# Routed stage: expert masks of chunks 1 to 3 spread by DMA instead of by TensorE and ScalarE, and the one-hot transposes moved to the turn before

## What is computed

```python
logits = gelu(xf @ w_r1 + b_r1) @ w_r2 + b_r2          # 8 experts
top_p, top_i = top_k(softmax(logits), 2)               # two experts a token
for _ in range(2):
    ctx = concatenate([integrated, v])                 # 256 features
    hidden = gelu(ctx @ expert_w1[i] + expert_b1[i])   # 64 wide, for each chosen expert
    ctrl = hidden @ expert_w2[i] + expert_b2[i]        # alpha, beta, gate: 3 x 128
    x_r, v_r = step(ctrl, integrated, v, mu)           # weighted by top_p, and summed
    ...                                                # the same for a shared expert; mixed
    integrated = integrated + halt * refined * integration_weight
```

## Time and profile before

| | us |
|---|---|
| median of 3 runs | 866.23 (865.97 to 867.63) |
| the profiled execution, its own time | 868.9 |
| its span, first to last instruction | 867.1 |
| PE busy in the span | 828.4 (96%) |
| DVE busy | 630.4 (73%) |
| ACT busy | 567.4 (65%) |
| GpSimd (POOL) busy | 286.4 (33%) |

### The profile page before, as it was taken

One profiled execution on the slowest core, in us unless ns is written; L12 is line 12 of the kernel. 1 busy time (PEld: TensorE's weight loads), 2 busy tenths in 40 slices (PEclk: granted clock), 3 DMA queues, 4 the chain that ended last, 5 costly groups with the idle time before them and its releaser, 6 DMA issues.

```text
span 867.1 us, 20115 instructions
## 1 busy us (share of the span) xinstructions
PE 828.4 (96%) x7204; PEld 571.1 (66%) x7204; DVE 630.4 (73%) x1587; ACT 567.4 (65%) x1569; POOL 286.4 (33%) x586
## 2 busy tenths in 40 slices
PE   9999999999999999999999999999999989899986
PEld 8887888888889976544444444444467665676652
DVE  5677776777776655685785766775989876789876
ACT  3666677677777676866545586445477779677664
POOL 4355444444554442200000000002156520334355
PEclk9999999999999999999999999999999999999999
DMA  8700000000000000000000000000000000000000
GB/s 340 156 2 2 1 2 1 2 2 1 2 1 2 2 1 2 1 1 0 1 0 1 0 1 0 1 0 1 1 27 3 4 3 1 2 4 3 3 15 37
DMA packets 7821, 13.55 MB, mean 16 GB/s; under 512 B 4342, under 2 KB 5036, under 8 KB 7468
## 3 DMA queue, kind: packets, MB, share of 16 engines
q1 hardware_dynamic: 7724, 12.27, 4.5%
HBM read 11.22 MB, written 1.05 MB: 14 GB/s over the span
## 4 chain that ended last, share of the span: by engine, by line
PE 59%; DVE 20%; POOL 10%; issue 6%; ACT 4%; DMA 0%; DVEq 0%; POOLq 0%; SPq 0%; ACTq 0%
PE psum L1551 10%; PE psum L767 6%; POOL rstd L515 4%; PE psum L807 4%; DVE arena L2083 3%; PE psum L750 3%; PE psum L759 3%; POOL arena L1095 2%; DVE negmax L1005 2%; PE psum L835 2%; PE psum L1560 2%; PE psum L1978 2%; ACT arena L905 2%; PE psum L2367 2%; PE psum L1570 2%
## 5 line engine op out<-in xcount | busy, mean ns | idle before, releaser
L512 POOL TENSOR_TENSOR ve<-mv,epsv 128x1 f32<-128x1 f32 x176 | 36.3, 206 | 462.1 <-DVE mv L507 462.1
L1551 PE MATMUL psum<-arena,w1f 128*128 128x512 f32 x240 | 109.5, 592 | 0.0
L515 POOL TENSOR_TENSOR rstd<-ve,epsv 128x1 f32<-128x1 f32 x176 | 101.2, 575 | 13.8
L905 ACT ACTIVATE arena<-psum,negmax 128x128 f32<-128x128 f32 x256 | 90.5, 407 | 22.2 <-DVE negmax L1005 22.2
L1551 PEld LDWEIGHTS psum<-arena,w1f 128*128 128x128 f32 x240 | 45.5, 190 | 49.9 <-issue 46.1
L1095 POOL TENSOR_TENSOR arena<-arena,rsum 128x512 f32<-128x512 f32 x64 | 65.2, 1039 | 5.6 <-DVE rsum L1011 5.6
L905 ACT ACTIVATION_READ_ACCUMULATOR arena<-psum,negmax 128x1 f32 x256 | 63.2, 247 | 0.0
L1005 DVE TENSOR_REDUCE negmax<-psum 128x8 f32<-128x1024 f32 x32 | 39.2, 1225 | 32.9 <-PE psum L807 32.9
L750 PE MATMUL psum<-arena,sclA 128*128 128x128 f32 x512 | 62.5, 275 | 0.1
L767 PE MATMUL psum<-arena 128*128 128x512 f32 x128 | 61.2, 598 | 0.7 <-DVE arena L1000 0.4
L807 PE MATMUL psum<-arena 128*128 128x128 f32 x512 | 59.9, 275 | 0.0
(11 more groups left out here) (371 smaller groups left out, 1995.7 us busy)
## 6 DMA issues: line engine op xcount, KB each, us to landing
w<-in_w0qk SPq DMA_DIRECT2D x2, 512.0 KB, 4.6
w<-in_w0vo SPq DMA_DIRECT2D x1, 1024.0 KB, 7.3
cT<-in_cT SPq DMA_DIRECT2D x1, 1024.0 KB, 16.7
out<-x_tok SPq DMA_DIRECT2D x4, 256.0 KB, 2.2
rows<-in_rows SPq DMA_DIRECT2D x1, 836.0 KB, 12.3
x_tok<-in_x_tok SPq DMA_DIRECT2D x1, 768.0 KB, 9.4
ctx_tok<-in_ctx_tok SPq DMA_DIRECT2D x1, 768.0 KB, 10.8
wa<-in_wa SPq DMA_DIRECT2D x1, 768.0 KB, 18.5
```

The lines of the kernel that those rows point to most:

```text
L515: pool.tensor_tensor(rstd[:, u, self.i:self.i + 1], ve[:, u, self.i:self.i + 1], epsv[:, 1:2], ALU.pow) \
L905: m = nc.scalar.activation(e0[:, b, g, :], ps(k, P, j * P), ACT.Exp, bias=negmax0[:, b, g:g + 1], accum_out=sum0[:, b, g:g + 1])
L1551: nc.tensor.matmul(ps(k), w1("e2", j * 384 + arg * D, j * 384 + (arg + 1) * D), f1_Hm[:, n, 2 * j + i, :], start=False, stop=False)
```

## The change

For the chunks 1 to 3 the step M is gone from the lists of PE and ACT. In its place the SP queue waits until `f1_ohT` of the chunk is stored, and issues 14 DMAs: each reads one row of `f1_ohT` (one partition, 512 bf16, 1 KB) and writes it to 64 partitions of a mask. The first 8 count on `f1_spread0`, the other 6 on `f1_spread1`; DVE step M waits for the whole first group with the masks A0 to B1, for the whole second group with A2, B2 and AB. Chunk 0 keeps its products and copies. Step O of chunk c moves from the head of turn (c,0) into the turn before, right after X GATE on PE and after C GATE on ACT (for chunk 1 to the end of the hand-written lists). Two anchors of the mixed-in tile steps move from M to H.

```diff
         def pe_turn(new, old, routed, ended):
+            routed_o = [("O", routed, 0, None)] if routed else []
...
-            order = first + (at("O") if new[1] == 0 and new[0] else []) + at("H", 0) + at("H", 1)
+            order = first + at("H", 0) + at("H", 1)
             order += [("L", 0, 0, None)] + at("H", 2) + at("H", 3) + at("H", "s") + [("R", 1, 0, None)] + at("O") if first else []
-            if new[1] == 0:
+            if first:
                 order += at("M", "A0") + at("M", "B0")
...
             if new[1] == 0:
-                order += of("ha") + of("G") + at("W") + at("B", GATE) + at("X", GATE)
+                order += of("ha") + of("G") + at("W") + at("B", GATE) + at("X", GATE) + routed_o
             else:
-                order += at("B", GATE) + at("X", GATE) + of("ha") + of("G") + at("B", ALPHA) + at("X", ALPHA)
+                order += at("B", GATE) + at("X", GATE) + routed_o + of("ha") + of("G") + at("B", ALPHA) + at("X", ALPHA)
...
         def act_turn(new, old, routed, ended):
...
-            if new[1] == 0:
-                order = first + (at("O") if new[0] else []) + at("H", 0) + at("H", 1) + at("M", "A0") + at("M", "B0") + at("H", 2) + at("M", "A1")
+            if first:
+                order = first + at("H", 0) + at("H", 1) + at("M", "A0") + at("M", "B0") + at("H", 2) + at("M", "A1")
...
-                order += of("ha") + at("D") + at("W") + routing + at("C", GATE)
+                order += of("ha") + at("D") + at("W") + routing + at("C", GATE) + routed_o
             else:
-                order += at("D") + routing + at("C", GATE) + of("ha") + (of("G") if scaled_by_act(*old) else []) + at("C", ALPHA)
+                order += at("D") + routing + at("C", GATE) + routed_o + of("ha") + (of("G") if scaled_by_act(*old) else []) + at("C", ALPHA)
...
-                  of_first("X", GATE), front("l1", 15)]
+                  of_first("X", GATE), front("l1", 15), ("O", 1, 0, None)]
...
-                   of_first("D", 12), of_first("W"), of_first("C", GATE), front("l1", 15)]
+                   of_first("D", 12), of_first("W"), of_first("C", GATE), front("l1", 15), ("O", 1, 0, None)]
...
-            at = {"pe": [(("H", 1), "pt", old), (("H", 2) if new[1] else ("M", "B0"), "att", old), (("H", "s") if new[1] else ("M", "AB"), "ou", old), (("B", BETA), "l2", old),
+            at = {"pe": [(("H", 1), "pt", old), (("H", 2), "att", old), (("H", "s"), "ou", old), (("B", BETA), "l2", old),
...
+        f1_spread = [sem(f"f1_spread{i}") for i in range(2)]
+        FIRST = 4
...
+        def mask_rows(arg):
+
+            slot, j = (0, 0) if arg == "AB" else (E * "AB".index(arg[0]), int(arg[1]))
+            return (0, 2 * E - 1) if arg == "AB" else (slot + 2 * (j + 1), slot + 2 * j + 1)
+
+        def sp_spread_masks(sp):
+            for c in range(1, N1):
+                t, n = At(c), c % 2
+                stored(sp, f1, "oh", t)
+                if c >= 2:
+                    sp.wait_ge(f1_masked, masked(c - 2, 1, MASKS[-1]))
+                for i, arg in enumerate(MASKS):
+                    for r, row in zip(SIDE.values(), mask_rows(arg)):
+                        sp.dma_start(f1_mask[n][i][r, :], f1_ohT[row:row + 1, n, :].unsqueeze(1).to_broadcast((1, HE, C1))) \
+                            .then_inc(f1_spread[i // FIRST], 16)
...
-                if it == 0:
+                if it == 0 and c == 0:
                     dve.wait_ge(f1_kept, held(c, arg))
+                elif it == 0:
+                    dve.wait_ge(f1_spread[i // FIRST], 32 * c * (len(MASKS) - FIRST if i >= FIRST else FIRST))
...
+        sp_parts.append(sp_spread_masks)
         sp_parts.append(sp_load_later)
```

## The result

The changed kernel takes 896.0 us (median of 4 runs, 895.7 to 896.6) against 866.4 in the same comparison (866.2 in the runs shown before): a ratio of 1.0337 (1.0323 to 1.035), 3.4% slower. The prediction was 907 with a range of 870 to 945. The profiled execution took 896.3 us, its span 894.5. In the later comparisons, beside the experiments, the kernel before had medians of 867.5 to 867.7. One of the 13 executions of e11 took 1644 us for a reason that no row shows, and its ratio leaves it out.

The account below looks back on a forecast made before the run. It took DVE's chain, not PE, to be last at the heads of the turns; transfers and O's wait added 34 us, the clock 7, so +41: 910 profiled, 907 predicted after 2.7 over the median, range 870 to 945.

Parts of the forecast that it names:

- DVE, not PE, ends the heads of the turns: Heads of (1,0), (2,0), (3,0): DVE's chain of the old pair is last; the mask products fill time PE would wait.
- the removed work is worth 0.5 us: Turns (1,0) and (2,0): without M AB ahead of `ou`, F comes 0.23 us earlier twice, -0.5 us.
- The faster rival: PE, not DVE, ends the turns: 21 products come off the path, 4.8 us, giving 861.4 us; chance 6%.
- O of chunk 2 waits 4.4 us for K: Turn (1,1): PE stands 4.4 us for weights from DVE's step K, work behind it queued; F 3.9 us late.
- The price of a transfer, p = 1.6 us between 0.6 and 2.6: Each one-row DMA: 0.6 if issue sets the pace, 2.6 if one engine reads the partition; 1.6 taken as middle.
- 12.7 and 14.2: Delays in us of the third product of slot A in B BETA from waiting for all 14 transfers, chunks 1 and 3.
- Chunk 2, +7.2 by its transfers: Turn (2,0): M A2 waits for all 14 transfers, done at 501.7 against 494.5; +7.2 us, containing the 3.9 from O.
- The clock, +7 for four stretches: PE's longer waits cause four stretches of 3.4 us at half clock, 1.7 us each; +7 us, bounds nothing and 10.
- The band of my forecast: Price of a transfer between 1.1 and 2.1 us gives 888 to 929 us; chance 52%.
- Issue-paced: Many readers of one partition don't disturb each other, 0.6 us a transfer; only O's wait remains: 870 to 877; chance 25%.
- one row at a time: Transfers don't overlap, 2.4 to 2.6 us each, giving 940 to 949 us; chance 15%.
- The signs: Profile after: PE idle some 4 us before chunk 2's O, DVE waiting on DMA before M, 1 KB packets far over 41 ns.

Follow-up runs that it names:

- e11: Kernel before, with DVE's step `att` moved ahead of M A0 in turns (1,0) and (2,0); 867.1 us, ratio 0.9987.
- e7: Changed kernel without its 42 transfers and their waits, chunk 0's masks used throughout, O of chunk 2 back at the head of (2,0); 870.9 us, ratio 1.0029.
- e9: Changed kernel with 18 small products without use on PE ahead of its wait for the weights of O of chunk 2; 895.0 us, ratio 1.0321.
- e5: Kernel before, with only step O of chunk 2 moved behind X GATE on PE and C GATE on ACT in turn (1,1); 874.8 us, ratio 1.0072.
- e1: Changed kernel with each transfer reading 64 partitions of the other parity's mask, not one row 64 times; 877.3 us, ratio 1.0103.
- e4: Changed kernel with all 14 transfers of a chunk reading row 0; 944.6 us, ratio 1.0871.
- e6: Changed kernel without its 42 transfers and the waits for them, chunks 1 to 3 using chunk 0's masks; 877.8 us, ratio 1.0111.

## Why the prediction held, and where it was off

- **DVE, not PE, ends the heads of the turns; the removed work is worth 0.5 us.** Held: e7 shows 0.2 us in all three turns, and idle time of PE where the products were; e11 gains what a shorter chain of DVE should give. The faster rival is refuted.
- **O of chunk 2 waits 4.4 us for K; F comes 3.9 us late.** The wait was 4.0 and the mechanism held (e9: F 4.4 late with the clock up). The move by itself costs 7.1 (e5), because the clock's share, which I had booked as a term of its own, falls on `ha` and G.
- **The price of a transfer, p = 1.6 us between 0.6 and 2.6.** The mis-sized term: it is 1.32. Both ends were found by experiment, 0.64 with a wide source and 2.30 with one row. With 1.32 in the same sums chunk 1 gives 374.0 + 1.9 + 18.5 + 0.7 - 386.3 = +8.8 (8.9 measured) and chunk 3 +10.3 (10.2), where 1.6 gave 12.7 and 14.2. One of the rows behind p was read too simply: the window at 31 us has, beside the loads into 64 partitions, some of 32 KB into all 128, so its half rate was weaker support than it seemed.
- **Chunk 2, +7.2 by its transfers.** The number was right for a wrong reason: with p at 1.32 the transfers land in time, and the 7.3 are the wait for O (4.4) and the clock (2.9). That the two sums agree is luck.
- **The clock, +7 for four stretches.** 2.9 in chunk 2 and 2.0 in chunk 3; in chunk 1 the half clock lay beside the wait for A2 and cost nothing.
- **The sum.** 34.1 + 7 became 23.5 + 4.9. Of the 12.7 us less, 10.6 are p and 2.1 the clock's count. Another 1.0 is the difference ahead of and behind the stage, and 2.4 go the other way, since the profiled execution lay 2.7 over the median before (866.2) and 0.3 after: that makes the 11 us between 907 and 896. The band of my forecast was added up a little wrong as well: p = 1.1 gives 890, not 888.
- **The rivals.** Issue-paced fell with e1, one row at a time with the kernel after against e4.
- **The signs.** The wait of O of chunk 2 for L1703 (now L1723) is there with 4.0 us, the packets take 0.21 us in the mean and not 0.04, and DVE waits for DMA ahead of the first M of chunk 1, 6.1 us where I wrote 8, and ahead of the fifth M of chunks 1 and 3. In chunk 2 that last wait, which I had announced for each chunk, is missing.

## What to carry to other kernels

Before work is taken off the busiest engine, look which engine releases it at that place: here PE's mask products filled a wait for VectorE, and taking them out gave at most 0.1 us a turn, while it left PE idle, and in e6 its clock fell there. A DMA that fans one SBUF row out to many partitions is paid at the source: price it by what is read, not by the bytes or the issues, and let neighbouring transfers read rows that do not stand in each other's way (here a copy 64 partitions further helped, one 32 further did not). And a step that is moved ahead in an in-order queue waits there for its operand with everything behind it; look up when the operand is ready before moving.

## What the runs showed of the hardware

- A DMA that reads one SBUF partition over and over moved 27 GB/s with the DMA engines busy 0.82 of the time; rows that change with each transfer (0 to 15, as in the kernel after) gave 51; reading every other one from a copy 64 partitions further gave 69, from one 32 partitions further still 51; 64 source partitions gave 103.
- PE's clock stood at 0.50 for 10.1, 6.7 and 13.5 us in and behind waits of 8.6, 4.0 and twice some 4 us, and with waits of 2.4 and 2.5 us ahead of F in turns (1,0) and (3,0) it fell in one execution (e6) and not in another with the same waits (e7). At 353 to 357 us it fell in eight of fourteen profiled executions and not in the others. Which executions lose it I cannot tell from these runs.
